# Layer 0's attention of a two-layer decoder block: half by half, with biases as products of a row of ones

## The chip, the cores and the metric

One core of a Trainium2 chip runs the whole program in one launch. The metric is the device time in microseconds (us), and less is better. A profiled execution gives a trace beside it: the engines are PE (TensorE), DVE (VectorE), ACT (ScalarE), POOL (GpSimd) and SP (SyncE, which here only issues DMAs).

## The reference

Input x is 4 batches of 256 tokens of width 256. Layer 0 is a linear attention of 16 heads, a cross-expert network of 4 experts chosen by token number (called x0 here) and a gated mixture of 8 experts (f0); layer 1 is a grouped softmax attention, a cross attention over a context, and a mixture of 8 experts with two shared ones (f1). Behind each comes a residual add and a layer norm. What the change touches is the first:

```python
q = _heads(hidden_states @ q_w.T + q_b, b, s)
k = _heads(hidden_states @ k_w.T + k_b, b, s)
v = _heads(hidden_states @ v_w.T + v_b, b, s)
qp = jax.nn.elu(q) + 1.0
kp = jax.nn.elu(k) + 1.0
kv = jnp.einsum('bhsd,bhse->bhde', kp, v)
z = jnp.einsum('bhsd,bhd->bhs', qp, kp.sum(axis=2))[..., None]
attn = jnp.einsum('bhsd,bhde->bhse', qp, kv) / (z + EPS)
out = attn.transpose(0, 2, 1, 3).reshape(b, s, HID)
return out @ o_w.T + o_b
```

and then x = layernorm(x + out). Float32 throughout.

## The kernel before

**Numbers.** Each large product is made of three: both operands are split into a high part, rounded to the matmul's fast float32 format, and a low part, the rest (`_hi`, `_lo`; ACT makes the high part with a copy, DVE or POOL the low part with a subtraction). High by high, high by low and low by high are summed in PSUM. PSUM has eight banks of 128 x 512 values.

**Tiling.** The 1024 tokens are 8 tiles of 128, in two halves h of 4 tiles (2 batches each). The width is KC = 2 chunks of 128. A half is 512 columns.

**The first stage** is written out by hand on each engine, ahead of the loops over the order lists. On SP, the transposed x and the weights of layer 0 are loaded (L312 to L327), then seven small or later loads on one semaphore, `in_small`. PE runs in this order: keys and values of half 0 (`a0_keys_values`, 24 products), queries of half 0 (`a0_query`, 12), keys and values of half 1, the state k'v of half 0 (`a0_state`), queries of half 1, q times state of half 0 (`a0_attend`), state of half 1, transposes of half 0 (`a0_transpose`), attend of half 1, output product of half 0 (`a0_project`), transposes and output product of half 1, then the transposes of the normed half 0 (L426), with which the experts of x0 begin. DVE adds the biases of keys and values from rows that a DMA has spread over the 128 partitions (L1289, L1290), computes elu + 1 in several steps (L1297, L1298, L1304, L1307), masks the state (L1316, L1317), divides (L1326 to L1332), makes the low parts (L1341), and adds the residual (L1349) into x_tok, to which POOL has added the output bias (L1086). DVE waits for all of `in_small` before its first bias add. ACT takes the exponentials (L871, L874), POOL splits weights.

**The rest** is five lists of steps, one for each engine (`SP_ORDER`, `PE_ORDER`, `ACT_ORDER`, `POOL_ORDER`, `DVE_ORDER`), which each engine runs in order and which meet through semaphores. Of the PE: `g`, `u`, `d` are gate, up and down products of an expert chunk (L414 to L417, L622 to L624). Of ACT: `s` silu, `h` high part of the hidden values, `G`/`D` high parts of gate/up and of down weights, `S` those of layer 1's attention weights and contexts. Of POOL: `l` low part of the hidden values, and `G`, `D`, `S` the low parts. Of DVE: `m` product of gate and up, `a` the weighted add of an expert's output into x_tok (L1412), `c` later constants. `n` are steps of the norm behind the attention, `r` those of f0's routing, `a0.`/`a1.` those of layer 1's attention for half 0/1. A bank is taken again only when its reader has signalled, so d waits for the adds of the d before (`acc_done`).

Of the kernel before, what the change touches and what calls it, by code (L numbers as in the profile page):

```python
# [7 lines left out]
F32 = mybir.dt.float32  # L8
# [8 lines left out]
P = 128  # L17
# [3 lines left out]
KC = D // P  # L21
# [21 lines left out]
CONST_W = P + BLK + GS + 8 + QH  # L43

# [61 lines left out]
g0 g1 g2 g3 n1.2 d0 g4 g5 d1 g6 g7 g8 d2 g9 d3 g10 g11 d4 g12 r0.2 g13 g14 d5 r0.3 g15 g16 u16 d6 g17 u17 g18 d7 u18  # L106
g19 u19 d8 g20 u20 r1.2 g21 u21 r1.3 d9 g22 u22 g23 d10 u23 g24 u24 g25 u25 d11 g26 u26 g27 u27 d12 g28 u28 g29 d13
u29 g30 u30 g31 u31 d14 d15 g32 u32 g33 u33 a0.2 g34 a0.3 a0.4 u34 g35 a0.5 a0.6 a0.7 d16 a0.8 u35 g36 u36 g37 u37 d17
a0.10 g38 u38 a0.25 g39 u39 a0.11 d18 a0.26 g40 u40 g41 d19 u41 g42 u42 a0.14 g43 u43 a0.15 d20 g44 a0.16 u44 g45
a0.17 u45 g46 a0.18 u46 d21 g47 u47 a0.21 d22 a0.22 d23 g48 u48 g49 u49 a1.2 g50 a0.24 a1.3 a1.4 u50 g51 a1.5 a1.6  # L110
a1.7 u51 a1.8 d24 g52 d25 u52 d26 d27 a1.10 g53 u53 a1.25 d28 a1.11 g54 a1.26 u54 g55 u55 g56 d29 u56 a1.14 g57 d30
a1.15 u57 d31 a1.16 d32 g58 a1.17 u58 g59 a1.18 u59 g60 d33 u60 g61 a1.21 d34 u61 a1.22 g62 u62 g63 d35 d36 d37 a1.24
u63 g64 u64 g65 d38 u65 g66 d39 u66 g67 d40 u67 g68 d41 u68 g69 d42 u69 g70 d43 u70 g71 d44 u71 g72 d45 u72 g73 d46
u73 g74 u74 g75 d47 u75 d48 d49 d50 d51
""".split()
ACT_ORDER = """
s0 h0 s1 n1.1 h1 s2 G0 h2 s3 n1.2 h3 D0 s4 h4 S0 s5 h5 s6 h6 s7 h7 s8 h8 s9 h9 s10 h10 s11 r0.1 h11 s12 r0.2 h12 s13
# [12 lines left out]
D3 G4 l22 D4 G5 l23 l24 l25 D5 G6 l26 D6 l27 G7 l28 S1 l29 D7 l30 l31 G8 S2 a0.0 D8 G9 D9 l32 G10 l33 l34 a0.7 D10  # L130
a0.8 l35 G11 D11 l36 G12 l37 l38 l39 D12 G13 a0.12 l40 a0.13 D13 G14 l41 l42 D14 G15 l43 l44 l45 S3 a0.19 D15 l46 l47
G16 D16 G17 D17 G18 a1.0 D18 G19 D19 S4 l48 l49 G20 l50 a1.7 a1.8 l51 D20 G21 D21 l52 l53 G22 D22 G23 D23 G24 D24
a1.12 l54 a1.13 G25 l55 D25 l56 G26 D26 G27 l57 D27 G28 D28 G29 l58 a1.19 D29 l59 G30 l60 D30 G31 l61 D31 G32 D32 G33
D33 l62 l63 G34 l64 D34 G35 l65 D35 G36 y0 l66 D36 G37 l67 D37 G38 l68 D38 G39 l69 D39 G40 l70 D40 G41 l71 D41 G42 l72
D42 G43 l73 D43 l74 l75 y1
""".split()
DVE_ORDER = """
n1.0 m0 m1 m2 m3 a0 n1.2 m4 a1 m5 m6 m7 a2 m8 m9 a3 r0.0 m10 a4 m11 m12 r0.2 m13 a5 m14 r0.3 m15 r0.4 a6 m16 r0.5 m17
a7 m18 r1.0 a8 m19 r1.2 m20 m21 r1.3 a9 r1.4 m22 a10 m23 m24 m25 r1.5 a11 m26 c m27 a12 m28 a13 m29 m30 m31 a14 a15
a0.0 m32 a0.2 m33 a0.3 a0.4 m34 a0.5 a0.6 a0.7 a0.8 m35 a16 a0.9 m36 a0.10 a17 m37 a0.25 m38 m39 a0.11 a18 a0.26 m40  # L140
a0.12 a19 m41 a0.14 m42 a0.15 m43 a20 a0.16 m44 a0.17 m45 a0.18 a0.19 a21 m46 m47 a0.21 a22 a0.22 a23 a0.23 a1.0 m48
a1.2 m49 a1.3 a1.4 m50 a1.5 a1.6 a1.7 a1.8 o51 m51 a1.9 o52 a1.10 m52 a1.25 o53 m53 a1.11 a1.26 o54 m54 a1.12 o55 m55
a1.14 o56 m56 a1.15 o57 m57 a1.16 o58 a1.17 m58 a1.18 a1.19 o59 m59 o60 m60 a1.21 o61 m61 a1.22 a1.23 m62 x0 m63 y0
m64 o65 m65 o66 m66 o67 m67 o68 m68 o69 m69 o70 m70 o71 m71 o72 m72 o73 m73 o74 m74 o75 m75 x1 y1
# [3 lines left out]
def decoder_program(nc, x_rows, x_cols, ids, pad_mask, w_attn0, w_attn1, bias_cols, bias_rows,  # L148
                    w_route, temperature, consts, pk_x0, pk_f0, pk_x1, pk_f1, out):
    with ExitStack() as ctx:  # L150
# [3 lines left out]
        def sem(name):  # L154
# [16 lines left out]
        kv_buf = sb("kv_buf", [P, TILES * D + TILES * KC * (P + 1)])  # L171
# [27 lines left out]
        headmask = con[:, P:2 * P]  # L199
        head8 = con[:, 2 * P:2 * P + HC]  # L200
# [17 lines left out]
        mhalf = sb("mhalf", [P, HT])  # L218
        mx = sb("mx", [P, TILES, HEADS])
# [178 lines left out]
        def _(pe):  # L398
# [38 lines left out]
            def a0_query(h):  # L437

                for c in range(KC):
                    for kc in range(KC):  # L440
                        m = split_mm(bank[2 * h + c][:, :], wa(kc, c * P, (c + 1) * P),
                                     (x_half(xT_hi, kc, h), x_half(xT_lo, kc, h)), kc == 0, kc == KC - 1)
                    m.then_inc(sems["a0_q_ps"], 1)

            def a0_keys_values(h):

# [1288 lines left out]
```

## Time and profile before

| | us |
|---|---|
| runs of the kernel before | 481.63, 480.71, 481.43, median 481.43 |
| the profiled execution, whole | 479.34 |
| its span, first to last instruction | 477.6 |
| mean granted clock of TensorE in it | 0.975 |
| PE, DVE, ACT, POOL busy in the span | 430.1, 256.4, 238.8, 264.5 |

The profiled execution is 0.4% under the median of the runs. Its span is 1.7 us less than its time.

### The profile page before, as it was taken

To read this page: it belongs to the slowest core of one execution; us is meant where nothing else is said; L and a number is where in the kernel's file an instruction comes from. 1 tells how busy PE (TensorE), PEld (TensorE's weight loads), DVE (VectorE), ACT (ScalarE), POOL (GpSimd) and SP (SyncE) were. 2 spreads that over 40 slices of the span, in tenths; PEclk is the share of its full clock that TensorE was granted. 3 is DMA by queue.
4 is the path that set the end of the run, shared out by engine and by line. 5 is a ranking of instruction groups with operands and counts; after the bars stand their busy time and mean duration, and the time that the engine had idled before them with its cause. 6 is when DMAs were issued, how large, how long until landed. Compare 5 with 4: busy or idle time off the path is not lost.

```text
span 477.6 us, 9222 instructions
## 1 busy us (share of the span) xinstructions
PE 430.1 (90%) x3642; PEld 363.4 (76%) x3642; DVE 256.4 (54%) x644; ACT 238.8 (50%) x401; POOL 264.5 (55%) x216
## 2 busy tenths in 40 slices
PE   2976789999999699899999998799989999999992
PEld 1866678988898588688897897588758888888882
DVE  2597654668655935346535668345525655522232
ACT  4122474575585145534636766533626756564431
POOL 1321378462866486915758465815275655876641
PEclk9999889999999799999999999999989999999997
DMA  7301213010321222400321122200241311433101
GB/s 257 121 35 77 106 33 106 0 45 23 109 68 67 67 92 91 139 33 23 109 95 63 36 87 78 77 2 1 80 134 47 115 40 44 138 135 109 47 1 44
DMA packets 15595, 35.51 MB, mean 74 GB/s; under 512 B 1984, under 2 KB 5824, under 8 KB 15552
## 3 DMA queue, kind: packets, MB, share of 16 engines
q1 hardware_dynamic: 15552, 34.92, 21.8%
q8 instruction: 29, 0.48, 0.4%
q14 instruction: 14, 0.11, 0.1%
HBM read 33.34 MB, written 1.05 MB: 72 GB/s over the span
## 4 chain that ended last, share of the span: by engine, by line
PE 66%; DVE 16%; ACT 5%; POOL 4%; issue 4%; SPq 3%; DMA 2%; ACTq 0%; DVEq 0%; POOLq 0%
PE bank L414 12%; PE bank L415 10%; PE bank L417 10%; PE bank L622 7%; PE bank L624 7%; PE bank L623 7%; ACT x_tok L847 2%; DVE stats L1206 2%; PE bank L579 2%; PE bank L696 2%; PE bank L641 1%; POOL rstd L1066 1%; PE bank L684 1%; DMA mask_w<-pad_mask_dram 1%; PE bank L426 1%
## 5 line engine op out<-in xcount | busy, mean ns | idle before, releaser
L1104 POOL TENSOR_TENSOR h_lo<-hraw,h_hi 128x512 fp32r<-128x512 f32 x76 | 98.2, 1293 | 78.8 <-ACT h_hi L906 78.4
L414 PE MATMUL bank<-xT_hi,pk_hi 128*128 128x512 f32 x256 | 106.5, 416 | 9.6 <-DVE hraw L1398 5.6
L415 PE MATMUL bank<-xT_hi,pk_lo 128*128 128x512 f32 x256 | 102.3, 400 | 0.0
L906 ACT ACTIVATE h_hi<-hraw 128x512 fp32r<-128x512 f32 x76 | 47.8, 629 | 73.0 <-DVE hraw L1398 72.9
L622 PE MATMUL bank<-pk_hi,h_hi 128*128 128x256 f32 x272 | 78.1, 287 | 5.1 <-DVE x_tok L1412 5.1
L417 PE MATMUL bank<-xT_lo,pk_hi 128*128 128x512 f32 x256 | 81.3, 399 | 0.0
L1398 DVE TENSOR_TENSOR hraw<-bank,sil 128x512 f32<-128x512 f32 x76 | 52.3, 688 | 50.3 <-PE bank L417 23.6
L1110 POOL TENSOR_TENSOR pk_lo<-pk_raw,pk_hi 128x512 fp32r<-128x512 f32 (+1 forms) x44 | 74.3, 1689 | 7.6 <-ACT pk_hi L924 7.5
L623 PE MATMUL bank<-pk_lo,h_hi 128*128 128x256 f32 x272 | 77.1, 283 | 0.0
L624 PE MATMUL bank<-pk_hi,h_lo 128*128 128x256 f32 x272 | 77.0, 283 | 0.0
L414 PEld LDWEIGHTS bank<-xT_hi,pk_hi 128*128 128x128 f32 x256 | 48.8, 190 | 26.4 <-issue 8.9
L1115 POOL TENSOR_TENSOR pk_lo<-pk_raw,pk_hi 128x256 fp32r<-128x256 f32 (+1 forms) x44 | 41.4, 940 | 30.5 <-ACT pk_hi L935 30.4
L417 PEld LDWEIGHTS bank<-xT_lo,pk_hi 128*128 128x128 f32 x256 | 48.8, 191 | 12.0 <-DVE xT_lo L1223 0.3
L622 PEld LDWEIGHTS bank<-pk_hi,h_hi 128*128 128x128 f32 x272 | 52.3, 192 | 7.3 <-issue 5.9
L415 PEld LDWEIGHTS bank<-xT_hi,pk_lo 128*128 128x128 f32 x256 | 49.0, 191 | 9.0
L935 ACT ACTIVATE pk_hi<-pk_raw 128x256 fp32r<-128x256 f32 (+1 forms) x44 | 21.7, 493 | 67.2 <-PE bank L624 67.1
L623 PEld LDWEIGHTS bank<-pk_lo,h_hi 128*128 128x128 f32 x272 | 52.5, 193 | 1.4
L624 PEld LDWEIGHTS bank<-pk_hi,h_lo 128*128 128x128 f32 x272 | 52.4, 193 | 0.0
L894 ACT ACTIVATE sil<-bank 128x512 f32<-128x512 f32 x76 | 44.9, 590 | 11.5 <-PE bank L417 11.3
L924 ACT ACTIVATE pk_hi<-pk_raw 128x640 fp32r<-128x640 f32 (+1 forms) x44 | 37.2, 846 | 8.1 <-PE bank L417 6.6
L847 ACT ACTIVATE x_tok<-x_tok,shift,rstd 128x256 f32<-128x256 f32 x48 | 24.9, 589 | 24.1 <-POOL shift L1067 24.1
L1412 DVE SCALAR_TENSOR_TENSOR x_tok<-bank,gold,x_tok 128x256 f32<-128x256 f32 x64 | 27.4, 476 | 11.9 <-PE bank L624 11.8
(212 smaller groups left out, 708.2 us busy)
## 6 DMA issues: line engine op xcount, KB each, us to landing
pk_raw<-pk_f_dram SPq DMA_DIRECT2D x28, 448.0 KB, 3.2
pk_raw<-pk_f_dram SPq DMA_DIRECT2D x16, 512.0 KB, 3.4
pk_raw<-pk_f_dram SPq DMA_DIRECT2D x16, 256.0 KB, 2.7
kv_buf<-pk_x_dram SPq DMA_DIRECT2D x4, 512.0 KB, 3.5
q_buf<-x_cols_dram SPq DMA_DIRECT2D x2, 512.0 KB, 6.3
x_tok<-x_rows_dram SPq DMA_DIRECT2D x1, 1024.0 KB, 10.0
pk_raw<-pk_x_dram SPq DMA_DIRECT2D x4, 256.0 KB, 4.3
out_dram<-x_tok SPq DMA_DIRECT2D x4, 256.0 KB, 2.7
```

What stands on the lines that cost most here:

```text
L414: pe.matmul(o, w(kc)[0], x(kc)[0], start=kc == 0, stop=False)
L415: pe.matmul(o, w(kc)[1], x(kc)[0], start=False, stop=False)
L417: m = pe.matmul(o, w(kc)[0], x(kc)[1], start=False, stop=kc == KC - 1)
L622: pe.matmul(o, hh, vh, start=closed and kc == 0, stop=False, skip_group_check=not closed)
L623: pe.matmul(o, hh, vl, start=False, stop=False, skip_group_check=not closed)
L624: m_ = pe.matmul(o, hl, vh, start=False, stop=closed and kc == chunks - 1, skip_group_check=not closed)
L894: A(sil[:, s % 2, :], src[:, :], ACT.Silu).then_inc(sems["silu_done"], 1)
L906: A(h_hi[:, row, at * 512:(at + 1) * 512], hraw[:, s % 2, :], ACT.Copy).then_inc(sems["hid_hi"], 1)
L1104: pool.tensor_tensor(h_lo[:, row, q], hraw[:, s % 2, :], h_hi[:, row, q].bitcast(F32), ALU.subtract).then_inc(sems["hid_lo"], 1)
L1110: pool.tensor_tensor(g_part(kind, i, pk_lo)[:, 0:w], raw_g(kind, i)[0][:, 0:w], g_part(kind, i, pk_hi)[:, 0:w].bitcast(F32), ALU.subtract) ...
L1115: pool.tensor_tensor(d_part(kind, i, pk_lo), raw_d(kind, i)[0], d_part(kind, i, pk_hi).bitcast(F32), ALU.subtract).then_inc(sems["d_lo"], 1)
L1398: TT(hraw[:, r, :], other[:, :], sil[:, r, :], ALU.mult).then_inc(sems["hid_mul"], 1)
```

## The change

**Steps.** The first stage becomes steps of the order lists: `b0.0` to `b0.9` and `b1.0` to `b1.9` for the two halves: 0 and 1 keys and values, 2 and 3 the queries of a chunk, 4 and 5 the state of a batch, 6 and 7 attend for a batch, 8 transposes, 9 output product. `p` are preparations (biases, splits of weights, the second half of x, constants), `X` the splits of x0's four packs, `v` the ones of layer 1's values.

**Biases.** A row of ones (33 partitions, rows 0, 1 and 32 set to 1) times a 33-row bias matrix (high part in row 0, 1.0 for the keys in row 1, low part in row 32) is one more product for each tile of keys and values and one for each tile of the output product. The bank so holds k + b + 1, and elu + 1 becomes max(min(exp(bank - 1), 1), bank): one ACT and one DVE instruction for each tile. ACT copies the values out of the bank. ACT makes relu(q + b), too. The state's mask gets 136 columns, so that one DVE instruction does a batch.

**Loads.** x and the key/value weights come in two chunks of the contraction each, the weights, bias rows and bias columns through ACT's queue. The small loads have semaphores of their own; five remain on `in_small`, behind the first two packs of x0.

**Warm-up.** PE begins with ten products of a tile of zeros.

**Order of the rest.** All five lists are new; steps move by a few places, layer 1's `S` splits by more.

```diff
 PE_ORDER = """
-g0 g1 g2 g3 n1.2 d0 g4 g5 d1 g6 g7 g8 d2 g9 d3 g10 g11 d4 g12 r0.2 g13 g14 d5 r0.3 g15 g16 u16 d6 g17 u17 g18 d7 u18
+b0.0 b0.1 b0.2 b0.3 b0.4 b0.5 b0.6 b0.7 b1.0 b0.8 b1.1 b0.9 b1.2 b1.3 b1.4 b1.5 b1.6 b1.7 n0.2 b1.8 g0 g1 b1.9 g2 g3
+d0 g4 n1.2 g5 g6 d1 g7 g8 d2 g9 g10 d3 g11 g12 d4 g13 r0.2 d5 g14 r0.3 g15 g16 u16 d6 g17 d7 u17 g18 u18 g19 u19 d8
...
 ACT_ORDER = """
+p0 p1 b0.0 b0.1 b0.2 b0.3 p2 p3 p4 X0 X1 b0.8 X2 X3 b1.0 b1.1 b1.2 b1.3 n0.1 n0.2 b1.8 G0 D0 s0 h0 s1 h1 s2 h2 s3 n1.1
...
 POOL_ORDER = """
+p1 p3 p4 X0 X1 X2 X3 n0.0 v0 G0 D0 l0 l1 n1.0 l2 l3 l4 l5 l6 l7 l8 l9 r0.0 l10 l11 l12 G1 D1 l13 l14 l15 l16 l17 G2
...
+r1.0 l18 l19 l20 D2 G3 D3 G4 l21 l22 D4 G5 l23 l24 l25 D5 G6 l26 l27 D6 G7 l28 D7 l29 G8 l30 l31 D8 G9 a0.0 D9 S0 l32
+G10 l33 S1 S2 l34 a0.7 a0.8 l35 D10 G11 D11 l36 G12 l37 l38 l39 D12 G13 a0.12 l40 a0.13 D13 G14 l41 l42 D14 l43 l44
...
 DVE_ORDER = """
+p0 b0.0 b0.1 b0.2 b0.3 b0.4 b0.5 p2 b0.6 b0.7 p5 b0.8 b1.0 b1.1 n0.0 b1.2 b1.3 b1.4 b1.5 b1.6 b1.7 n0.2 b1.8 m0 m1
+n1.0 m2 m3 a0 m4 n1.2 m5 m6 a1 m7 m8 a2 m9 m10 a3 r0.0 m11 a4 m12 r0.2 m13 a5 m14 r0.3 m15 r0.4 a6 m16 r0.5 m17 a7 m18
...
@@ SP
+            for c in range(KC):
+                sp.dma_start(q_buf[:, c, 0:512], xc[:, c, 0:512]).then_inc(sems[f"in_xT{c}"], 16)
+            sp.dma_start(wa_raw[:, :, 0:D], w_attn0[:, :, 0:D]).then_inc(sems["in_w0_q"], 16)
+            sp.dma_start(q_buf[:, :, 512:1024], xc[:, :, 512:1024]).then_inc(sems["in_xT2"], 16)
...
@@ PE
+                ones_b = lambda t: pe.matmul(kv_bank(h, t)[:, :], ones_r, b_kv, start=False, stop=True)
...
+            def a0_state(h, b):
+                pe.wait_ge(sems["a0_eq"], KC * h + b + 1)
+                pe.wait_ge(sems["a0_kp"], HT * h + 2 * b + 2)
+                pe.wait_ge(sems["a0_v"], HT * h + 2 * b + 2)
...
+            pe.wait_ge(sems["ones_ready"], 1)
+            for _ in range(WARM):
+                pe.matmul(bank[3][:, :], zero_r[:, 0:P], zero_r[:, :], start=True, stop=True)
@@ ACT
+            for c in range(KC):
+                act.dma_start(wa_raw[:, c, D:3 * D], w_attn0[:, c, D:3 * D]).then_inc(sems[f"in_w0_k{c}"], 16)
+            act.dma_start(brow[0:BZ, :], bias_rows).then_inc(sems["in_bz"], 16)
+            act.dma_start(bcol[:, :], bias_cols).then_inc(sems["in_bcol"], 16)
...
+                        A(v_buf[:, T, :, 0:P], kv_bank(h, t)[:, D:2 * D].rearrange("p (c d) -> p c d", c=KC), ACT.Copy
+                          ).then_inc(sems["a0_v"], 1)
+                        A(ek[:, T, :], kv_bank(h, t)[:, 0:D], ACT.Exp, bias=mone[:, 0:1]).then_inc(sems["a0_ek"], 1)
...
+                    A(eq[:, c, q], q_bank(h, c)[:, :], ACT.Exp, bias=bcol[:, c:c + 1])
+                    A(q_buf[:, c, q], q_bank(h, c)[:, :], ACT.Relu, bias=bcol[:, c:c + 1]).then_inc(sems["a0_eq"], 1)
@@ POOL
-            pool.tensor_tensor(x_tok[:, :, :], x_tok[:, :, :],
-                               brow[:, 2 * D:3 * D].unsqueeze(1).to_broadcast([P, TILES, D]), ALU.add
-                               ).then_inc(sems["a0_xb"], 1)
@@ DVE
+                STT(k_tok[:, T, :], ek[:, T, :], 1.0, kv_bank(h, t)[:, 0:D], ALU.min, ALU.max).then_inc(sems["a0_kp"], 1)
...
+                    TT(state[:, n:n + KC, :], q_bank(h, b)[:, :].rearrange("p (c n) -> p c n", c=KC)[:, :, 0:BLK],
+                       headmask.unsqueeze(1).to_broadcast([P, KC, BLK]), ALU.mult).then_inc(sems["a0_state"], 1)
```

## Rows read from the trace of the kernel before

**Rows 1.** Stretches: from:to, length, busy us (count) by engine, granted clock, DMA.
```profile
30.00:40.00 10.00, 7.19 (x57) 6.59 (x56) 9.82 (x28) 3.81 (x8) 4.07 (x4) 1.00 0.33 126
40.00:50.00 10.00, 6.60 (x47) 6.19 (x47) 6.77 (x22) 2.12 (x4) 0.72 (x1) 0.90 0.01 6
```

**Rows 2.** Chain that ended last: start us, length us, what.
```profile
16.96 0.42 DVE kv_buf L1289
...
49.12 1.42 DVE stats L1206 x4
```

**Rows 3.** Timeline of the first loads: start, length, engine, what, idle before.
```profile
5.21 1.06 ACT L852 ACTIVATE xT_hi<-q_buf 128x1024 fp32r<-128x1024 f32 x1 [3.19 <-DMA q_buf<-x_cols_dram]
...
9.33 0.77 PE L454 MATMUL bank<-wa_hi,xT_hi 128*128 128x512 f32 x1 [9.33 <-DVE wa_lo L1277]
```

**Rows 4.** PE's timeline, four starts: products of 512 columns at either pace.
```profile
12.45 0.63 PE L455 MATMUL bank<-wa_hi,xT_lo 128*128 128x512 f32 x1
12.88 0.63 PE L456 MATMUL bank<-wa_lo,xT_hi 128*128 128x512 f32 x1
...
14.48 0.40 PE L455 MATMUL bank<-wa_hi,xT_lo 128*128 128x512 f32 x1
14.71 0.39 PE L456 MATMUL bank<-wa_lo,xT_hi 128*128 128x512 f32 x1
```

**Rows 5.** Groups, 0 to 62 us: form, count, busy us, mean ns, idle before.
```profile
L480 PE MATMUL bank<-state,q_buf 128*128 128x136 f32 x32 | 4.1, 282 | 0.7 <-DVE state L1317 0.7
...
L1289 DVE TENSOR_TENSOR kv_buf<-bank,brow 128x256 f32<-128x256 f32 x8 | 3.3, 413 | 3.9 <-DMA mask_w<-pad_mask_dram 3.9
...
L1332 DVE TENSOR_TENSOR kx<-bank,rs 128x256 f32<-128x256 f32 x8 | 2.8, 416 | 0.1
...
L1298 DVE SCALAR_TENSOR_TENSOR kv_buf<-kv_buf,kx 128x1024 f32<-128x1024 f32 x2 | 2.5, 1225 | 0.1
...
L883 ACT ACTIVATE h_hi<-bank 128x512 fp32r<-128x512 f32 x4 | 2.2, 594 | 11.4 <-PE bank L489 11.4
...
L1075 POOL TENSOR_TENSOR wa_lo<-pk_raw,wa_hi 128x512 fp32r<-128x512 f32 x2 | 2.5, 1270 | 18.9 <-ACT wa_hi L858 18.9
```

**Rows 6.** Timeline around the norm of half 0 and x0's first products.
```profile
51.28 1.02 POOL L1066 TENSOR_TENSOR rstd<-var_e,mhalf 128x4 f32<-128x4 f32 x1 [10.56 <-DVE var_e L1212]
...
55.85 0.47 PE L414 MATMUL bank<-xT_hi,pk_hi 128*128 128x512 f32 x1 [0.67 <-ACT xT_hi L840]
...
56.22 1.28 ACT L894 ACT_TABLE_LOAD   x1
...
61.09 0.47 PE L414 MATMUL bank<-xT_hi,pk_hi 128*128 128x512 f32 x1 [2.10 <-DVE hraw L1398]
...
71.93 0.28 PE L622 MATMUL bank<-pk_hi,h_hi 128*128 128x256 f32 x1
```

**Rows 7.** Timeline: one DVE operation in either half's routing, and POOL beside it.
```profile
115.80 0.19 DVE L1446 TENSOR_TENSOR fb<-fb,none_in 128x32 f32<-128x32 f32 x1
...
156.45 2.30 DVE L1446 TENSOR_TENSOR fb<-fb,none_in 128x32 f32<-128x32 f32 x1
...
156.32 2.39 POOL L1110 TENSOR_TENSOR pk_lo<-pk_raw,pk_hi 128x1024 fp32r<-128x1024 f32 x1
```

**Rows 8.** PE's longest wait behind it, and a stretch as in Rows 1.
```profile
162.11 0.55 PE L622 MATMUL bank<-pk_hi,h_hi 128*128 128x256 f32 x1 [4.02 <-DVE x_tok L1412]
...
164.00:168.00 4.00, 4.00 (x20) 3.92 (x20) 3.60 (x7) 0.34 (x1) 0.78 (x1) 0.57 0.00 0
```

**Rows 9.** POOL in layer 1's attention: two splits, an idle time, and a load (KB, us to landing).
```profile
L1121 POOL TENSOR_TENSOR wa_lo<-kv_buf,wa_hi 128x1536 fp32r<-128x1536 f32 x1 | 3.5, 3501 | 0.1
...
L1125 POOL TENSOR_TENSOR xp_lo<-kv_buf,xp_hi 128x1024 fp32r<-128x1024 f32 x4 | 9.6, 2396 | 0.4 <-ACT xp_hi L948 0.2
...
208.30 1.29 POOL L1104 TENSOR_TENSOR h_lo<-hraw,h_hi 128x512 fp32r<-128x512 f32 x1 [5.79 <-ACT h_hi L906]
...
kv_buf<-pk_x_dram SPq DMA_DIRECT2D x4, 512.0 KB, 3.5
```

More of the change, by code:

```diff
@@ L139 @@
[L139 to L143, printed above, removed]
@@ new lines, in a0_query @@
+            def a0_query(h, c):
+                if h == 0 and c == 0:
+                    pe.wait_ge(sems["wa_lo_done"], 1)
+                elif c == 0:
+                    pe.wait_ge(sems["a0_kp"], HT + 2)
+                    pe.wait_ge(sems["a0_v"], HT + 2)
+                for kc in range(KC):
+                    m = split_mm(q_bank(h, c)[:, :], wa(kc, c * P, (c + 1) * P),
+                                 (x_half(xT_hi, kc, h), x_half(xT_lo, kc, h)), kc == 0, kc == KC - 1)
+                m.then_inc(sems["a0_q_ps"], 1)
@@ L876, in _ @@
-            w_high("o", slice(3 * D, 4 * D))
-            A(rw[:, :, :, 0, :], rw_raw[:, :, :].rearrange("p c (r e) -> p c r e", e=E0), ACT.Copy
-              ).then_inc(sems["small_ready"], 1)
-            x0_high(0)
-            for h in range(2):
-                for c in range(KC):
-                    act.wait_ge(sems["a0_aT_ps"], KC * h + c + 1)
-                    A(h_hi[:, h, c * 512:(c + 1) * 512], bank[2 * h + c][:, :], ACT.Copy).then_inc(sems["a0_aT_hi"], 1)
-                x0_high(1 + h)
@@ L1293, in a0_key_features @@
-            def a0_key_features(h):
-                ks, es = (b[:, HT * h:HT * (h + 1), :].rearrange("p t d -> p (t d)") for b in (k_tok, ek))
-                dve.wait_ge(sems["a0_ek"], h + 1)
-                link(TS(es, es, 1.0, None, ALU.min))
-                STT(ks, ks, 0.0, es, ALU.max, ALU.add).then_inc(sems["a0_kp"], 1)
-            def a0_query_features(h):
-                q = slice(h * 512, (h + 1) * 512)
-                for c in range(KC):
-                    dve.wait_ge(sems["a0_eq"], KC * h + c + 1)
-                    m = TS(q_buf[:, c, q], bank[2 * h + c][:, :], bcol[:, c:c + 1], 0.0, ALU.add, ALU.max)
-                link(m)
-                for c in range(KC):
-                    STT(q_buf[:, c, q], eq[:, c, q], 1.0, q_buf[:, c, q], ALU.min, ALU.add).then_inc(sems["a0_q"], 1)
@@ L1309, in a0_state @@
-            def a0_state(h):
-                for b in range(2):
-                    dve.wait_ge(sems["a0_st_ps"], 2 * h + b + 1)
-                    for c in range(KC):
-                        n = KC * (2 * h + b) + c
-                        src = bank[2 * h + b]
-                        TT(state[:, n, 0:P], src[:, c * 256:c * 256 + P], headmask, ALU.mult)
-                        m = TS(state[:, n, P:BLK], head8, src[:, c * 256 + P:c * 256 + P + 1], None, ALU.mult)
-                    m.then_inc(sems["a0_state"], 1)
```

502 lines of the change are left out of this document (290 added, 212 removed).

## The prediction

> **What bounds the kernel now.** I read the busy times of stretches first, then the chain that ended last, then the timeline of the first 80 us, and last PE's waits behind it. From 20 us on, DVE is the full engine of the attention stage: from 30 to 40 us it is busy 9.82 of 10 us and PE 7.19; from 40 to 50 us both fall under 7 [rows 1]. The chain says the same: from DVE's first bias add at 16.96 us to the statistics of the norm at 49.12 us it is nearly all DVE [rows 2]. The bias add sat idle for 3.9 us until a small late load (the mask) had landed, though the product it reads was there [rows 5]. PE began at 9.33 us, with x landed at 5.2 us [rows 3], and its products started 0.43 us apart at 12.5 us and 0.23 us apart at 14.5: the levels of 1.2 and 2.4 GHz [rows 4]. x0's first gate product starts at 55.85 us, the third waits 2.10 us, and the second down product starts at 71.93 us [rows 6]. Behind that point PE is the bound, but for some waits, the longest of 4.02 us [rows 8]. So what the change is worth is how much earlier PE reaches the second down product (6 gate products, both transposes, one down product done), and then what the new order of the rest does.
>
> **Costs of one operation.** A 512-column product 0.23 us, at the low level 0.43 [rows 4]; of 256 columns half of that; eight pieces of state or attend for a batch 1.0 (4.1 us for 32) [rows 5]. DVE on 256 columns of a bank 0.35 to 0.41 [rows 5]. The new key operation (min, max) is not in the trace: a quarter of the 1024-wide one is 0.31, the bias add 0.41; I take 0.40, as it reads a bank. The one masking operation of 272 columns: 0.37, by the 256-wide divide. ACT on 512 columns of a bank takes 0.59, 0.54 from start to start; on 256 columns lies between half and all of that, 0.27 to 0.54; I take 0.40, and at 0.54 a tile's two ACT operations (1.1 us) would just outlast PE's 0.93 a tile and add 0.6 us.
>
> **The change, half 0.** The first 512 KB (now x chunk 0 and key/value chunk 0, on two queues) land as before at 5.2 us; ACT 0.55, DVE 0.6: PE starts at 6.2 instead of 9.33. Twelve products of chunk 0 end at 9.0; for chunk 1 and the bias product the tiles are done at 10.2, 11.1, 12.0, 13.0. Here DVE begins its tiles, 6.7 us earlier than the 16.96. Queries: PE to 15.8, ACT (two operations each) to 17.0, DVE to 17.7. State products run inside that, masks to 18.5, attend to 20.1, DVE's split of x half 1 to 19.8, its divides to 22.7.
>
> **Half 1 in between.** PE goes on with half 1's keys and values (20.1 to 23.4), half 0's transposes (24.4), the rest of the keys and values (27.7), half 0's output product with four bias products (3.2 us, to 30.9), half 1's queries (33.7). DVE adds the residual and has the statistics at 33.7. State and attend of half 1 take until 38.1, as ACT's last relu (35.0) and DVE's masks come in turn. Meanwhile POOL (1.3) and ACT (2.1) have normed half 0 at 37.2. Transposes of half 0 end at 39.0, of half 1 at 40.4, held by DVE's last divide at 40.05. g0 starts at 40.4 (55.85 before), g1 ends at 43.3. ACT's table load of 1.28 us [rows 6] and the first silu lie beside half 1's output product (43.3 to 46.5), so that the 2.10 us before g2 go. g2 and g3 end at 49.3; d0 waits for POOL's low part until 49.7, ends at 52.5, g4 at 53.9. Half 1's norm is late next: statistics 51.2, POOL 52.6, ACT 55.2; its transposes hold PE for 1.3 us. g5 ends at 56.9. Before, the same was done at 71.93 [rows 6]: 15.0 us less.
>
> **What is added.** Eight bias products of 512 and eight of 256 columns: 1.9 + 0.9 us of PE, counted above. POOL loses its 2048-wide output bias add, which lay off the path. The ten products of zeros (4.3 us at the low level) start when POOL's two memsets are done, near 1.8 us, and end at 6.1, in PE's idle time; I count that the first true products then find the high level, as the products before did by 14.5 us, 5 us into their run [rows 3, 4]. ACT now issues four DMAs before its first copy; at 0.4 to 1.0 us each they end before x lands. `p4` makes ACT wait for the five small loads at 18.7 us; they come behind the same amount of loads as the one that landed at 16.9, plus 1 us; nothing is left if they are over 1 us later, and each us then moves all of half 1.
>
> **Collisions of DVE and POOL.** One DVE operation took 0.19 us in half 0's routing and 2.30 in half 1's, where it ended together with a POOL split that had started first (156.32 + 2.39) [rows 7]. My chain has DVE's operations with two operands in SBUF (x's split, the query features) near POOL's splits of 1.27 us [rows 5]. I count one met for 1.0 us; none is the lower end, five the upper (6.4 us). The Trainium skill (SBUF — State Buffer, section "Who interferes with whom") says that DVE with two SBUF inputs and a GpSimd operation that reads SBUF exclude each other for a whole instruction; the trace agrees. It speaks against putting POOL's splits beside the attention: by it alone, with all five met, the time is 5.4 us over my forecast.
>
> **The rest of the lists** do the same operations in a slightly other order. No row says that it is better or worse; I count 0, with 5.7 us either way, the price of one such wait as the longest: 4.0 us and, in the 4 us behind it at a granted clock of 0.57, some 1.7 us [rows 8]. That wait came from the collision above, so it is luck of the order.
>
> **Sum.** 15.0 - 1.0 = 14.0 us. Against the profiled execution (479.3) that is 465.3; the runs' median is 481.4, 2.1 us above it, so I forecast **467.4**.
>
> **Rivals.**
> (A) The zeros don't bring the clock up, or it falls again before the first true product. Then 10 of the first products run 0.2 us slower: 469.4. For it: nothing in this trace shows how such products count; against it: PE fell to the low level only after it had waited.
> (B) The new order meets one more long wait like that of rows 8: 473.1. (C) It loses the one it has: 461.7. For C, `d11` is now later than `g27`, for B, `a11` still stands behind the routing on DVE.
> (D) Half 1 doesn't fill half 0's waits, because DVE or ACT is as full as before; both stay serial: 481. Against it: a half's DVE work falls from some 14 us to 9.
> (E) Slower than before: the one buffer for layer 1's weights and contexts. `S0`, `S1`, `S2` now stand on ACT and POOL right in the attention that needs them, and each load waits for the split before: 3.5, then twice 3.5 to land [rows 9], 1.0 on ACT and 2.4 on POOL = 17.3 us in a row, with ACT's silus queued behind, and 1.7 us of low clock: 19.0. If nothing covers it: 486.4. It decides from the point where less than 5.0 us of it are covered. Against it: POOL sat idle 5.79 us there [rows 9], and PE has four steps of 2.8 to 5.9 us (query and key products, d16, values) beside it, which cover most.
>
> **How the numbers follow.** Forecast (464 to 471) 0.52; A 0.10; B 0.15; C 0.13; D 0.03; E 0.07. The range goes to 460 (C, with no collision) and to 475 (B, with A or more collisions). Faster by over 0.2% (about what a measurement of this kernel can tell from no change) 0.90, same 0.03, slower 0.07.
>
> **What would show it.** Right: g0 near 40 us, second down product near 57, DVE's first key tile near 10.5, no gap above 1.5 us on PE between 6 and 57, product starts 0.23 us apart from the first key product on. A shows as 0.43 us there. B and C show as PE waits behind 57 us that are new or gone; E as PE waits before `a0.5` to `a0.10` with ACT's or POOL's split of the contexts as releaser. I am wrong if g0 starts after 45 us, or if ACT is the full engine from 15 to 35 us: then my 0.40 us for ACT on 256 columns is too low.

## The result

The changed kernel takes 466.5 us (median of 4 runs, 463.9 to 470.9) against 481.1 (480.4 to 481.6) for the kernel before beside it: a ratio of 0.968, 95% interval 0.965 to 0.971. One of the 4 runs, that of 470.9, was in a slower state, and every ratio here leaves such runs out. The forecast was 467.4. The total was right; two of its terms were wrong by 6.2 and 4.7 us, with opposite signs.

The profiled execution took 466.7 us, its span 464.9 (before: 477.6). First the same stretches as in [rows 1], and the two of the changed kernel in which the granted clock was low (columns as there):

```profile
30.00:40.00 10.00, 10.00 (x49) 7.14 (x48) 5.52 (x12) 4.28 (x12) 2.52 (x2) 1.00 0.46 157
40.00:50.00 10.00, 9.59 (x63) 8.03 (x62) 7.92 (x25) 7.54 (x14) 2.65 (x4) 1.00 0.24 82
...
232.00:236.00 4.00, 4.00 (x12) 3.15 (x12) 0.47 (x2) 0.60 (x1) 2.58 (x2) 0.59 0.81 219
288.00:292.00 4.00, 3.12 (x13) 2.48 (x12) 0.34 (x2) 2.77 (x8) 3.83 (x3) 0.66 0.28 49
```

From 30 to 40 us DVE falls from 9.82 to 5.52 us and PE rises from 7.19 to 10.00: the stage that DVE bound is now bound by PE. ACT is not full either (4.28 and 7.54 us of 10). That is what the change is for, and it works. PE's timeline of the start, of the first key and value tiles, and of the two places that [rows 8] and the collision term speak of:

```profile
1.52 4.64 PE L584 MATMUL bank<-zero_r 128*128 128x512 f32 x10 [1.52 <-POOL kv_buf L1162]
...
7.53 0.39 PE L466 MATMUL bank<-wa_hi,xT_hi 128*128 128x512 f32 x1
7.76 0.39 PE L467 MATMUL bank<-wa_hi,xT_lo 128*128 128x512 f32 x1
...
12.17 0.40 PE L479 MATMUL bank<-wa_lo,xT_hi 128*128 128x512 f32 x1
12.50 0.49 PE L460 MATMUL bank<-pr_hi,pr_lo 33*128 33x512 f32 x1
12.92 0.50 PE L477 MATMUL bank<-wa_hi,xT_hi 128*128 128x512 f32 x1
13.26 0.39 PE L478 MATMUL bank<-wa_hi,xT_lo 128*128 128x512 f32 x1
...
23.99 0.51 PE L495 MATMUL bank<-wa_hi,xT_hi 128*128 128x512 f32 x1 [0.74 <-DVE xT_lo L1345]
...
151.12 0.35 PE L679 MATMUL bank<-pk_hi,h_hi 128*128 128x256 f32 x1 [0.94 <-DVE x_tok L1490]
```

The true products run 0.23 us apart from 7.53 us on. But around the bias product (L460, the one of 33 rows) the starts are 0.33, 0.42 and 0.34 us apart, where 0.23 was counted each time. The wait of 4.02 us [rows 8] is one of 0.94.

Where the time went, at points at which PE has done the same steps in either order (gate and up products found by their instructions of L414 and L435; 65 is the first of g24):

| point | before | after | earlier by |
|---|---|---|---|
| start of the first gate product | 55.85 | 47.45 | 8.40 |
| end of the sixth gate product (g5), with transposes and first down product done | 71.93 | 64.56 | 7.37 |
| start of g24 (gate instruction 65) | 143.99 | 135.94 | 8.05 |
| start of u35 | 220.25 | 205.91 | 14.34 |
| end of the span | 477.6 | 464.9 | 12.7 |

So the stage gave 7.4 to 8.1 us, the lists between g24 and u35 gave 6.3, and behind that 1.6 us were given back. The forecast was 14.0 for the stage and 0 for the lists. The 1.6 us belong in part to this one execution: in another profile of the changed kernel (464.7 us, of the runs that stand beside experiment 5) the clock from 232 to 236 us is 1.00, and the lead over the kernel before is 14.2 us at u35 and 14.7 at the end.

### The profile page after: what moved, and what is told of

Read it like the earlier page. It is cut to its first block, busy times and chain, and to the rows that moved or that the text cites. A ratio compares the mean times of both kernels' runs of the same rounds, so it can differ in the third digit from the quotient of the medians.

```text
span 464.9 us, 9286 instructions
## 1 busy us (share of the span) xinstructions
PE 439.1 (94%) x3668; PEld 367.4 (79%) x3668; DVE 248.5 (53%) x625; ACT 247.2 (53%) x424; POOL 261.5 (56%) x217
## 4 chain that ended last, share of the span: by engine, by line
PE 56%; DVE 4%; ACT 3%; POOL 2%; issue 2%; ACTq 0%; POOLq 0%; DVEq 0%
PE bank L435 11%; PE bank L438 9%; PE bank L436 9%; PE bank L679 5%; PE bank L681 5%; PE bank L680 5%; PE bank L753 2%; PE bank L636 2%; PE bank L741 1%; DVE stats L1301 1%; ACT x_tok L905 1%; POOL rstd L1156 1%; PE bank L725 1%; PE bank L727 1%; PE bank L726 1%
## 5 line engine op out<-in xcount | busy, mean ns | idle before, releaser
L435 PE MATMUL bank<-xT_hi,pk_hi 128*128 128x512 f32 x256 | 106.1, 414 | 4.0 <-DVE hraw L1476 3.2
L435 PEld LDWEIGHTS bank<-xT_hi,pk_hi 128*128 128x128 f32 x256 | 48.7, 190 | 21.9 <-issue 8.8
L1456 DVE TENSOR_TENSOR sil<-bank,sil 128x512 f32<-128x512 f32 x22 | 15.2, 689 | 34.6 <-ACT sil L980 29.5
```

## Experiments

Three groups of four; each ratio is to the kernel before on the same chip (480.7, 480.8 and 480.5 us in the three groups). A step is named as in the order lists (g24 is gate product 24). Three questions: why the stage gave 6 us too little, what the lists did, and what PE's clock has to do with either.

**1. The bias products over all 128 rows.**

```diff
-        b_kv = pr_hi[0:BZ, :, :].rearrange("p t d -> p (t d)")
-        b_o = pr_lo[0:BZ, 0, :]
-        ones_r = pr_lo[0:BZ, 1, 0:P]
+        b_kv = pr_hi[:, :, :].rearrange("p t d -> p (t d)")
+        b_o = pr_lo[:, 0, :]
+        ones_r = pr_lo[:, 1, 0:P]
...
-            link(dve.memset(ones_r.bitcast(F32), 0.0))
+            dve.memset(pr_hi[:, :, :].bitcast(F32), 0.0)
+            link(dve.memset(pr_lo[:, :, :].bitcast(F32), 0.0))
```

> The changed kernel, but the sixteen bias products run over all 128 rows (rows 33 to 127 of both operands are set to zero once, by two DVE memsets), so the result is the same. Theory: in the changed kernel's trace a tile of keys and values takes 1.32 us instead of the 0.93 us of four products, because PE must finish one product before it takes weights of 33 rows, and again before it takes the next of 128; so 16 products cost 0.4 us too much each. Then tiles come every 0.93 to 1.0 us, g0 starts 4 to 6 us earlier (42 to 43 instead of 47.4), and the time falls by 4 to 6 us, to 461 to 463. Rival: it is the added product, not its number of rows; then the tile stays at 1.3 us and the time within 1 us of the changed kernel's 466.5.

Measured: 460.1 us (458.8 to 460.8), ratio 0.958 (0.955 to 0.961), 6.4 us under the changed kernel. The first gate product starts at 42.90 us and not at 47.45. The same products and the weight loads ahead of them, first of the changed kernel (two rows of PEld, two of PE), then of this one (one of PEld, four of PE):

```profile
12.49 0.18 PEld L460 LDWEIGHTS bank<-pr_hi,pr_lo 33*128 33x128 f32 x1 [0.37 <-issue]
12.92 0.19 PEld L477 LDWEIGHTS bank<-wa_hi,xT_hi 128*128 128x128 f32 x1 [0.24 <-issue]
...
33.80 0.38 PE L561 MATMUL bank<-pr_lo 33*128 33x256 f32 x1
35.02 0.38 PE L561 MATMUL bank<-pr_lo 33*128 33x256 f32 x1
```

```profile
11.89 0.19 PEld L460 LDWEIGHTS bank<-pr_hi,pr_lo 128*128 128x128 f32 x1
...
12.12 0.39 PE L460 MATMUL bank<-pr_hi,pr_lo 128*128 128x512 f32 x1
13.05 0.39 PE L460 MATMUL bank<-pr_hi,pr_lo 128*128 128x512 f32 x1
...
30.68 0.28 PE L561 MATMUL bank<-pr_lo 128*128 128x256 f32 x1
31.52 0.28 PE L561 MATMUL bank<-pr_lo 128*128 128x256 f32 x1
```

With 128 rows the weights load 0.23 us ahead of their product, while the one before it runs. Weights of 33 rows load only as their product starts (12.49 and 12.50), and so do the 128-row weights behind them (12.92 and 12.92). A tile of keys and values takes 0.93 us from bias product to bias product here (12.12 to 13.05) and 1.32 in the changed kernel (12.50 to 13.82, one tile on), one of the output product 0.84 and 1.22. That is 8 x 0.39 + 8 x 0.38 = 6.2 us for 16 bias products, beside their own 2.8; twelve of them lie ahead of the first gate product, which is 4.55 us earlier, and with all sixteen done g5 ends at 59.11 for 64.56, 5.45 us earlier. The rival, that the added product costs it whatever its rows, is out. The Trainium skill (TensorEngine Tiling (Array Packing), section "Tiling Modes", "Key Properties") says that a change of the tiling mode drains the array. The rows agree, in the missing load ahead and in the 0.10, 0.19 and 0.11 us lost ahead of the product, behind it and one product on; that a product of 33 rows is such a change, and that the loss is a drain, no run here shows.

**2. The warm-up left out.** `WARM = 0`.

> The changed kernel without the ten products of zeros. Theory: the first products from 6.6 us on start 0.43 us apart for some 4 us, so 9 or 10 of them cost 0.2 us more each, and the time is 1.5 to 2 us longer, 468 to 469. Rival: products of zeros don't bring the high level, or the stage has slack in it; then within 0.5 us of the changed kernel.

Measured: 467.7 us (465.3 to 468.7), ratio 0.974 (0.971 to 0.977). PE's first products:

```profile
7.29 0.63 PE L467 MATMUL bank<-wa_hi,xT_lo 128*128 128x512 f32 x1
7.71 0.63 PE L466 MATMUL bank<-wa_hi,xT_hi 128*128 128x512 f32 x1
...
11.34 0.39 PE L477 MATMUL bank<-wa_hi,xT_hi 128*128 128x512 f32 x1
```

They run 0.43 us apart from 7.29 to 10.3 and 0.23 from 11.34 on; with the zeros the quick pace is there at 7.53. So products of zeros bring the clock up as any others do. Their worth is 0.94 us at the first gate product (48.39 for 47.45; 0.76 against the changed kernel's other profile, 47.63), not the 2.0 of rival A nor the 1.5 to 2 expected; the medians are 1.2 us apart, and the runs of both kernels overlap. One reason: with the zeros, PE waits 0.50 us at 11.2 for the low part of the biases instead.

**3. The stage alone, and the lists alone.** The changed stage with its head of the lists, and the old order behind the head; and the other way round. Their edit is the five lists.

> The changed kernel's first stage and its lists up to the fifth gate product or so, and behind that the lists of the kernel before. Theory: the stage is worth 8 us (g0 at 47.45 instead of 55.85), the new order of the rest the other 4.7. Then 472 to 474. Rival: the rest only gains because the stage shifted it against the DMAs; then the time stays at 466 to 468, and the long wait near 150 us is gone here too.

> The kernel before with its own first stage and lists up to the fifth gate product or so, and behind that the order of the changed kernel. Theory: the long wait before the down product at 158 us is gone with the later down product (d11), 4 to 6 us; 475 to 477. Rival: the order brings nothing by itself; 480 to 482.

Measured: the stage alone 477.8 us (473.8 to 484.5), ratio 0.993 (0.989 to 0.996); the lists alone 474.0 (472.1 to 476.7), ratio 0.988 (0.984 to 0.991). The lists carry 6.7 us by themselves. With the lists alone the product of [rows 8] waits 1.07 us, and the clock stays up behind it:

```profile
159.73 0.35 PE L622 MATMUL bank<-pk_hi,h_hi 128*128 128x256 f32 x1 [1.07 <-DVE x_tok L1412]
...
160.00:164.00 4.00, 4.00 (x31) 3.73 (x30) 2.70 (x7) 2.96 (x5) 4.00 (x3) 1.00 0.56 147
```

From g24 to u35 PE needs 76.26 us before, 69.97 in the changed kernel, 69.56 with the new lists alone and 75.69 with the new stage alone (in the second profile of it, below). So some 6 us there are the lists'. The stage alone gave much less than its 8 us, and its profile was of the longest of its 12 executions (484.5 us), so it was run again:

> The changed stage with the orders of the kernel before behind it, once more, for a profile that can be read to the end: the first one ran at a lower clock in its last third. The theory that the stage's 8.4 us are kept up to 140 us and one us or two of them are lost at the wait near 155 and after: gate products 65 and 113 near 136.5 and 196, and 473.5 to 476 us in the profiled execution. The rival, that the order of before gives the stage's gain back behind 200 us: 477 to 480 us with a wait or a low clock there that the kernel before does not have.

Measured: 476.8 us (473.7 to 480.8), ratio 0.991 (0.989 to 0.994). It is ahead of the kernel before, which has the same order there, by 8.5 us at the first gate product, 7.1 at g24 (136.85), 7.8 at gate instruction 113 (195.43), 5.5 at g52 (323.60), and 1.6 at g56 (356.59). The theory's two early times were met, but for the whole the rival was right: the gain goes behind 200 us, most of it behind 320.

```profile
344.57 0.79 PE L435 MATMUL bank<-xT_hi,pk_hi 128*128 128x512 f32 x1 [2.15 <-POOL pk_lo L1196]
...
344.00:348.00 4.00, 3.42 (x48) 2.39 (x52) 0.00 (x0) 0.46 (x1) 4.00 (x5) 0.50 0.38 116
348.00:352.00 4.00, 4.00 (x107) 3.14 (x99) 1.38 (x3) 0.14 (x1) 2.31 (x3) 0.50 0.51 150
352.00:356.00 4.00, 4.00 (x14) 2.77 (x13) 1.94 (x5) 1.86 (x3) 2.52 (x2) 0.79 0.51 150
```

The kernel before has a wait of 2.32 us there too, but the clock is low for one such stretch only (0.57 from 348 to 352 us) and not for two and a half. In the changed kernel every 4 us from 320 to 364 have a clock of 1.00. So the two parts do not add up (3.7 + 6.7 = 10.4 us of 14.6): the stage keeps its last 4 us only with the new lists behind it. Why the low stretch is longer in one kernel than in the other after the same wait stays open. The length of the wait alone does not decide it: the same wait of 2.09 us for DVE's q_buf near 34 us leaves the clock at 1.00 in the profiles of the kernel before and of the lists alone, and at 0.84 and 0.73 from 32 to 40 us in those of experiments 4 and 7.

**4. Zeros in the one long wait of the kernel before.**

```diff
+                if u == 12:
+                    pe.wait_ge(sems["ones_ready"], 1)
+                    for _ in range(18):
+                        pe.matmul(bank[7][:, :], zero_r[:, 0:P], zero_r[:, :], start=True, stop=True)
                 if 1 <= u < U_F1:
                     pe.wait_ge(sems["acc_done"], 4 * u)
```

The zeros themselves are written at the start, by GpSimd, and no longer by DVE.

> The kernel before, with 18 products of zeros in TensorE's one long wait (4.02 us at 158 us, for VectorE's sum of x), ahead of the wait, into a bank that nothing reads. After that wait the granted clock was 0.57 over 160 to 168 us. The theory that the changed orders gained 6.4 us there in two halves, 3.1 us of the wait and 3.4 us of clock: the wait's end stays at 162 us, the clock stays at 1.00, and the time is 3 to 3.5 us under the kernel before, 477.3 to 478. The rival, that the clock is no part of it: within 0.5 us of the kernel before.

Measured: 478.7 us (median of 12: eleven from 477.7 to 480.2, and one of 619.9), ratio 0.996 (0.994 to 0.998).

```profile
158.52 4.27 PE L615 MATMUL bank<-zero_r 128*128 128x512 f32 x18
...
164.00:168.00 4.00, 4.00 (x26) 3.55 (x25) 3.93 (x8) 2.50 (x5) 2.52 (x2) 1.00 0.02 4
```

Nothing is done earlier, PE only isn't idle, and the clock that was 0.57 from 160 to 168 us is 1.00. From g24 to u35 it takes 73.84 us and not 76.26: 2.4 of the 6.3 us were clock and 3.1 the wait itself (4.02 less 0.94). The 0.8 left lie ahead of g34, where PE waited 0.99 us for POOL's pk_lo before and has no such wait in the changed kernel. (The first gate product came 0.84 us later than before, at 56.69, so the whole gained 1.8 and missed the expected 3. Whether the memset in its new place did that is not shown: the same stage began it at 55.12 to 55.88 in the other three profiles.)

**5. The halves in series.**

```diff
-b0.0 b0.1 b0.2 b0.3 b0.4 b0.5 b0.6 b0.7 b1.0 b0.8 b1.1 b0.9 b1.2 b1.3 b1.4 b1.5 b1.6 b1.7 n0.2 b1.8 g0 g1 b1.9 g2 g3
+b0.0 b0.1 b0.2 b0.3 b0.4 b0.5 b0.6 b0.7 b0.8 b0.9 b1.0 b1.1 b1.2 b1.3 b1.4 b1.5 b1.6 b1.7 b1.8 b1.9 n0.2 g0 g1 g2 g3
```

The same for ACT and DVE.

> The changed kernel with the two halves of layer 0's attention in series again: each engine's lists take the second half's steps behind the first half's, products, copies, sums, transposes and biases are the same ones. The theory that the interleaving is what hides the divides, the bf16 splits and the copies: TensorE waits again at each of them (divide and low part of the first half, some 2 to 3 us, and the same for the second), so the second half's first gate product comes 4 to 6 us later than the changed kernel's 47.45 us, and the whole is 470.5 to 472.5 us. The rival, that the stage is bound by TensorE's own products whatever their order: at most 1 us slower, 466 to 468 us.

Measured: 490.0 us (484.9 to 494.4), ratio 1.019 (1.015 to 1.023); the changed kernel beside it 466.1.

> The changed kernel as it is, for a comparison on the same chip with the series and the full rows. Every theory expects 466 to 467.5 us.

Measured: 466.1 us (463.7 to 468.5), ratio 0.969 (0.966 to 0.972). So the series is 24 us slower, not 4 to 6, and slower than the kernel before. (What the expectation calls bf16 splits are those into a high and a low part.) Its waits, and the two stretches at the low clock:

```profile
25.33 0.66 PE L544 MATMUL bank<-con,kx 128*128 128x128 f32 x4 [2.09 <-DVE kx L1408]
29.41 0.55 PE L558 MATMUL bank<-wa_hi,h_hi 128*128 128x256 f32 x1 [1.96 <-DVE h_lo L1446]
58.46 0.39 PE L558 MATMUL bank<-wa_hi,xp_hi 128*128 128x256 f32 x1 [1.90 <-DVE xp_lo L1446]
...
26.00:38.00 12.00, 9.71 (x33) 7.51 (x34) 3.84 (x14) 2.12 (x4) 3.11 (x3) 0.50 0.39 141
60.00:72.00 12.00, 11.44 (x38) 8.95 (x37) 1.33 (x3) 4.43 (x6) 2.42 (x2) 0.50 0.00 0
```

The waits are near what was expected (2.1 and 2.0 us, 0.5 and 1.9). What was not expected: PE ran at half clock for 12 us twice, from between the first two waits on and from behind the last, and was busy for 9.7 and 11.4 us of them.

**6. The series with zeros in its waits.**

```diff
+            def keep_busy(o, n):
+                for _ in range(n):
+                    pe.matmul(o[:, :], zero_r[:, 0:P], zero_r[:, :], start=True, stop=True)
+
             def a0_transpose(h):
+                keep_busy(bank[4 if h else 3], 2 if h else 9)
...
+                keep_busy(bank[4 if h else 3], 8)
                 pe.wait_ge(sems["a0_aT_lo"], KC * (h + 1))
```

> The series kernel, with products of zeros in TensorE's four waits inside it (9 ahead of the first half's transposes, 8 ahead of its output product, 2 and 8 in the second half), into banks that nothing reads; they end before the awaited values come, so no wait and no work is taken away. In the series kernel TensorE waited 2.10 us at 23.23, 1.95 at 27.46, 0.52 and 1.90 at 54 to 58, and the granted clock was 0.50 from 26 to 38 us and from 60 to 72. The theory that its 24 us over the changed kernel are some 8 us of waits and, above all, some 12 to 13 us of products at half clock after them: the clock stays at 1.00, the first gate product comes near 56 us and not at 68.21, and the time is 476 to 480 us against 490. The rival, that the series is slow for its waits alone and the clock follows something else: 488 to 491 us.

Measured: 478.6 us (476.6 to 482.6), ratio 0.996 (0.994 to 0.999): 11.4 us less than the series, for products that compute nothing.

```profile
22.88 2.33 PE L541 MATMUL bank<-zero_r 128*128 128x512 f32 x9
26.75 2.09 PE L541 MATMUL bank<-zero_r 128*128 128x512 f32 x8
...
24.00:32.00 8.00, 7.36 (x39) 5.21 (x38) 5.00 (x19) 2.12 (x4) 5.03 (x4) 1.00 0.23 66
```

So the interleaving's 24 us are 11.4 us of clock and 12.5 of the rest. Of those, 7.2 us are the waits (the zeros' own 2.33 + 2.09 + 0.72 + 2.09), and 2.5 are waits of 1.46, 0.67 and 0.36 us around the first gate products; some 3 us I can't place. The first gate product came at 60.56, 7.65 us ahead of the series, and not near 56: the last 4 us of the second low stretch lie behind it (it started at 68.21 in the series), so that only part of the 11.4 us is won by then. The Trainium skill (TensorE: Matmul & The Clock Gate, section "HAM oscillation — how this bites in real kernels") tells of a kernel in which the clock falls in each wait for a DMA, so that the next group of products starts at the low level. The trace of experiment 5 agrees, at waits for DVE of 2.1 and 2.0 us close together.

**7. The early biases alone.** In the kernel before, the constants' and biases' loads get a semaphore of their own.

```diff
-            sp.dma_start(brow[:, :], bias_rows.partition_broadcast(P)).then_inc(sems["in_small"], 16)
+            sp.dma_start(brow[:, :], bias_rows.partition_broadcast(P)).then_inc(sems["in_first"], 16)
...
-            dve.wait_ge(sems["in_small"], 16 * 7)
+            dve.wait_ge(sems["in_first"], 16 * 3)
```

> The kernel before with one thing changed: the loads of the constants and the biases have a semaphore of their own, and what uses the biases waits for those three loads and not for all the first small loads. The theory that the kernel before began late because its first bias sum waited for loads that it did not use (DVE's first sum at 16.96 us): the first bias sum comes near 12.7 us, TensorE's stage ends 2 to 4 us earlier, and the whole is 477 to 479 us. The rival, that the key and value products end at 17 us anyway and the sums then run back to back: within 1 us of the kernel before, 480 to 481.5 us.

Measured: 480.8 us, ratio 1.000 (0.997 to 1.002): nothing, although the first sum comes 4.6 us earlier.

```profile
12.34 0.42 DVE L1291 TENSOR_TENSOR kv_buf<-bank,brow 128x256 f32<-128x256 f32 x1 [1.01 <-DMA brow<-bias_rows_dram]
17.68 0.41 DVE L1292 TENSOR_TENSOR kv_buf<-bank,brow 128x256 f32<-128x256 f32 x1
19.29 2.09 DVE L1299 TENSOR_SCALAR kx<-kx 128x1024 f32<-128x1024 f32 x1 [1.19 <-ACT kx L871]
```

The fourth tile's sum still waits for PE, so 4.6 us have shrunk to 1.6 at the last sum (17.68 for 19.29), and a collision with GpSimd's sum (16.20 to 20.82 us) halves that (2.09 us for an operation that took 1.24 before); at the first gate product (55.88) nothing is left. The late load [rows 5] was the first wait of DVE's chain and not what bound it.

**8. DVE and POOL kept apart**, on the kernel of experiment 1.

```diff
+                    pool.wait_ge(sems["bz_lo"], 1)
...
+                    pool.wait_ge(sems["xt_lo"], 2 * KC)
```

> The kernel with the bias products over all 128 rows, and two waits more on GpSimd: its split of x's second half starts only once VectorE's low part of the biases is written, and its next split only once VectorE's split of x is done, so that the two engines do not run their long operations beside each other. The theory that each collision stretches VectorE's operation by about 1 us while TensorE waits for it: TensorE's gaps of 0.82 us at 11.12 and 0.7 us near 24 go, and the time is 1 to 1.5 us under the same kernel without these waits (460.1 us), 458.6 to 459.1. The rival, that the later splits delay the second half's products by as much as is won: no change, or up to 1 us slower.

Measured: 458.4 us (458.1 to 460.2), ratio 0.953 (0.951 to 0.956). The collision of the changed kernel, and below it the same two operations here:

```profile
21.58 2.36 DVE L1345 TENSOR_TENSOR xT_lo<-q_buf,xT_hi 128x512 fp32r<-128x512 f32 x2
21.57 1.82 POOL L1166 TENSOR_TENSOR wa_lo<-pk_raw,wa_hi 128x512 fp32r<-128x512 f32 x1 [10.78 <-ACT wa_hi L915]
```

```profile
19.35 1.28 DVE L1348 TENSOR_TENSOR xT_lo<-q_buf,xT_hi 128x512 fp32r<-128x512 f32 x2
20.71 1.29 POOL L1167 TENSOR_TENSOR wa_lo<-pk_raw,wa_hi 128x512 fp32r<-128x512 f32 x1 [9.57 <-DVE xT_lo L1348]
```

DVE's split (two operations of 512 columns) takes 1.28 us and not 2.36, and POOL's takes 0.5 less too; PE's waits at 11 and 24 us are gone, and the first gate product starts at 41.13 us, 1.77 ahead of experiment 1's. Apart from each other both engines are quicker, so the later start costs nothing.

**9. Zeros in the two longest waits of that kernel** (10 ahead of one product, 7 ahead of another, near 276 and 282 us).

> The fastest kernel so far (bias products over all rows, engines kept apart) with products of zeros in TensorE's two longest waits: 10 in the wait of 2.51 us at 275.73, 7 in the one of 1.69 us at 281.55. There the granted clock fell to 0.50 from 284 to 286 and was 0.69 from 286 to 288. The theory that the clock alone is lost there: 1 to 2 us faster than 458.4, 456.5 to 457.5. The rival, that the products after these waits hang on GpSimd and VectorE anyway: within 0.5 us of 458.4.

Measured: 457.8 us (456.1 to 458.4), ratio 0.952 (0.949 to 0.954). The stretch behind the waits, with and without them, in this order:

```profile
282.00:286.00 4.00, 3.71 (x17) 2.37 (x16) 1.48 (x4) 1.34 (x5) 1.67 (x2) 1.00 0.71 246
```

```profile
282.00:286.00 4.00, 2.77 (x9) 1.95 (x10) 1.48 (x4) 0.75 (x3) 1.18 (x1) 0.73 0.70 246
```

The clock's fall is gone, and from g46 to g52 PE needs 53.4 us for 54.6 (but experiment 1's kernel and the changed one need 53.4 there, too). But in the median it is 0.6 us, and the intervals overlap: not shown. It is the fastest kernel of the study, 8.3 us under the changed one and 22.7 under the one before.

## Why the prediction was right, and where it was not

**PE's start and the clock: right.** 6.2 us was counted and 6.60 measured; the zeros bring the clock up (experiment 2). Rival A is out, and even as an error it would have cost 0.8 to 0.9 us at the first gate product, not 2.0.

**The bias products: wrong, the largest miss.** The term was 1.9 + 0.9 us, 0.23 and 0.12 a product. It took them for products like their neighbours, though the diff shows 33 rows beside 128. They cost 9.0: 6.2 more (experiment 1). The price stood in the trace of the kernel before, in layer 1's products of 16 rows (L579): the next product starts 0.43 us behind one, and not 0.23:

```profile
339.53 0.50 PE L579 MATMUL bank<-cwT,pk_hi 16*128 16x512 f32 x1
339.96 0.51 PE L414 MATMUL bank<-xT_hi,pk_hi 128*128 128x512 f32 x1
```

There are 22 of these in the traces of both kernels and of the fastest one; at 0.39 us each they still cost some 8.6 us, an estimate from experiment 1 that no run tested.

The first key tile of DVE came at 12.49 and not near 10.5, the first gate product at 47.45 and not 40.4, over the line of 45 at which I called myself wrong. But ACT was not full, as that test would have had it: the 0.40 us for ACT on 256 columns held (0.38, and 0.47 for the exponential).

**The collisions: right in size, one too few.** One was counted at 1.0 us. Two were met: 1.52 us for an operation of 0.41 at 9.54, and 2.36 for 1.28 at 21.58, so 1.1 us each. Apart, they gave 1.8 us at the first gate product (experiment 8). With both causes taken away it starts at 41.13, 0.7 us from the chain's 40.4. The sixth gate product, whose end the chain put at 56.9, ends at 64.56 in the changed kernel and at 57.33 without the two causes. So the chain's other links held to within 1 us, and "a half's waits are filled by the other half" is shown, by more than was counted: experiment 5 put the step at 24 us, 11.4 of them clock. Rival D is out with that.

**The rest of the lists: wrong by 4.7 us.** 0 was counted; 6.3 us were won and 1.6 given back. It is rival C's mechanism, "it loses the one it has", with 0.13, and its price of 5.7 us (4.0 of wait and 1.7 of clock) was near the 6.3 found, though 0.94 of the wait stayed and the clock was worth 2.4. The prediction put the wait down to a collision of DVE and POOL, and the traces bear that out. Ahead of DVE's sum of x, first before (with [rows 7]), then in the changed kernel:

```profile
152.58 0.63 ACT L935 ACTIVATE pk_hi<-pk_raw 128x512 fp32r<-128x512 f32 x1 [3.60 <-PE bank L624]
153.88 1.26 DVE L1443 TENSOR_SCALAR s<-s 128x4 f32<-128x4 f32 x1
155.38 1.03 DVE L1445 TENSOR_TENSOR fb<-fb,s 128x32 f32<-128x32 f32 x1
```

```profile
147.34 0.19 DVE L1523 TENSOR_TENSOR fb<-fb,s 128x32 f32<-128x32 f32 x1
147.57 0.19 DVE L1524 TENSOR_TENSOR fb<-fb,none_in 128x32 f32<-128x32 f32 x1
148.88 0.63 ACT L1021 ACTIVATE pk_hi<-pk_raw 128x512 fp32r<-128x512 f32 x1 [5.15 <-PE bank L681]
149.58 1.28 POOL L1201 TENSOR_TENSOR pk_lo<-pk_raw,pk_hi 128x512 fp32r<-128x512 f32 x1 [5.02 <-ACT pk_hi L1021]
```

Three operations of DVE's routing take 1.26, 1.03 and 2.30 us before, beside POOL's splits, and 0.17, 0.19 and 0.19 in the changed kernel: 4.04 us, the whole wait. With the old lists on a stage 8 us earlier three of them take 1.00, 1.22 and 2.28, and the wait is 3.80; with the new lists on the old stage these are short, and it is 1.07. The 0.94 us left in the changed kernel go with one operation that still meets a split (1.26 us for 0.17, at 143.32). In the changed kernel POOL's splits start only behind the routing, because ACT makes the high part that they need once the down product `d11` has freed its place, and `d11` now stands behind `g27`. So the step that failed is "luck of the order", counted as 0: which splits lie beside the routing follows from the lists and could have been read off them. No run moved `d11` alone, so that it and no other entry does this is argued from the traces and not shown. **Rival E** is out: PE waits 0.84 us for DVE's q_buf in that attention, as before, and has no new wait with ACT's or POOL's split of the contexts as releaser. **Rival B** did not come: the longest new wait is one of 1.27 us at 231.82, ahead of the low clock there, for which the profile shows no other engine.

So the chain made 465.3 us of profiled time where 466.7 was measured: the stage fell short by some 6 us of its 14.0 (6.2 of bias products, of which 5.4 reached g5, and some 1 of a collision), and the lists gave 4.7. The 2.1 us added for the distance of the profiled execution to the median weren't there this time (466.7 against 466.5). The forecast of 464 to 471 with 0.52 was right about the number and not about the reasons.

## What to carry to other kernels

Put a small product among large ones in the large ones' form: fill the rows up with zeros, rather than switch to fewer rows and back (6.4 us here). Read a wait of PE with the stretch behind it: the four waits of the series cost more in clock (11.4 us) than in waiting (7.2), and zeros can fill a wait at no cost, if they go into a bank that is free and end before the wait does. A load or a sum that comes earlier is worth what is left of it at the next in-order wait, so follow it to the first product that needs it. And when a short operation of DVE takes 1 to 2 us, look at what POOL runs beside it and at which list entry puts it there.

## What the runs showed of the hardware

- A product of 33 rows between products of 128 costs 0.38 to 0.39 us over its own time, whether it has 512 or 256 columns: its weights and those of the next product aren't loaded ahead. Behind one of 16 rows the next starts after 0.43 us, too.
- Products of zeros count for the clock like others. After 10 of them (1.52 to 6.16 us) the true products were 0.23 us apart from the third on; without them 0.43 us for the first 3.6 us.
- At two waits of 2.1 and 2.0 us with 2 us between them the granted clock was 0.50 (1.2 GHz) over 12 us, with PE busy for 9.7 of them; around the one of 4.02 us in the kernel before it was 0.57 over 8 us. After a single one of 1.46 us, in experiment 6, it did not fall. After one of 2.09 us it fell in two profiles and not in two others.
- DVE and GpSimd slow each other, in both directions: 1.28 to 2.36 us, and 1.29 to 1.82. It held for small operations as well (256 elements on one partition, 0.41 to 1.52 us; 128 x 32, 0.19 to 2.30).
